# Graph attention sums: the value rows of all four heads are weighed by one VectorE operation, and ScalarE keeps only the exponentials

## The reference, cut to what matters

```python
m = jax.ops.segment_max(score, col_idx, num_segments=n)
ex = jnp.exp(score - m[col_idx])
denom = jax.ops.segment_sum(ex, col_idx, num_segments=n)
alpha = ex / denom[col_idx]
agg = jax.ops.segment_sum(alpha[..., None] * msg_edge, col_idx, num_segments=n)
```

## Time and profile before

| | us |
|---|---|
| median of 3 runs | 4174.1 (4173.09 to 4183.92) |
| the profiled execution's own time | 4177.06 |
| its span, first to last instruction | 4175.2 |
| PE busy | 3149.1 (75%) |
| DVE busy | 2234.4 (54%) |
| ACT busy | 894.9 (21%) |
| POOL busy | 2743.4 (66%) |

### The profile page before, as it was taken

How to read it: one execution, slowest core, us unless ns; L and a number is a source line. 1 busy time by engine, 2 the same in 40 slices (tenths; PEclk the granted TensorE clock), 3 DMA queues, 4 the chain that set the end, 5 groups by cost and what they waited for, 6 DMA issues and landing times. The chain is left out here.

```text
span 4175.2 us, 64203 instructions
## 1 busy us (share of the span) xinstructions
PE 3149.1 (75%) x11666; PEld 2153.8 (52%) x11666; DVE 2234.4 (54%) x7572; ACT 894.9 (21%) x2584; POOL 2743.4 (66%) x2879
## 2 busy tenths in 40 slices
PE   5999938777788873786788878888786776767763
PEld 2444426556566652333667767777544444444442
DVE  8200037666666646333788868776654433444435
ACT  1333300000200000342344456555320000100000
POOL 3777767777677775234777767777217777477774
PEclk9999959999999986998887769877888877788876
DMA  4333323333333334566555546555213333333332
GB/s 142 142 145 151 142 73 105 106 105 105 95 105 106 106 107 131 217 257 233 165 165 165 164 129 176 163 162 162 66 50 106 105 105 106 99 106 105 105 106 90
DMA packets 226896, 540.00 MB, mean 129 GB/s; under 512 B 73482, under 2 KB 107948, under 8 KB 212876
## 3 DMA queue, kind: packets, MB, share of 16 engines
q0 software_dynamic: 136528, 374.97, 30.1%
q1 hardware_dynamic: 57880, 103.46, 6.8%
q10 hardware_dynamic: 32164, 57.91, 4.7%
HBM read 390.04 MB, written 146.09 MB: 128 GB/s over the span
## 5 line engine op out<-in xcount | busy, mean ns | idle before, releaser
L604 POOL DMA_INDIRECT gcn_edges_g<-table,rows_i x782 | 740.3, 947 | 434.3 <-ACTq L875 196.7
L923 PE MATMUL ps<-gcn_edges_g,gcn_edges_onehot 128*128 x1760 | 627.8, 497 | 309.1 <-SPq L620 271.4
L969 DVE TENSOR_TENSOR acc<-acc,ps 128x256 f32 (+1 forms) x880 | 370.0, 420 | 750.6 <-PE ps L923 740.3
L923 PEld LDWEIGHTS ps<-gcn_edges_g,gcn_edges_onehot 128*128 128x128 f32 x1760 | 392.2, 242 | 537.3 <-issue 484.5
L307 POOL DMA_INDIRECT records<-rec,slots x391 | 375.9, 961 | 184.1 <-issue 124.2
L604 POOL DMA_INDIRECT score_g<-table8v,rows_i x391 | 380.2, 972 | 131.0 <-issue 110.6
L604 POOL DMA_INDIRECT rel_g<-table,rows_i x391 | 371.8, 951 | 134.7 <-issue 96.9
L604 POOL DMA_INDIRECT score_g<-table8k,rows_i x391 | 371.4, 950 | 135.0 <-issue 109.4
L604 POOL DMA_INDIRECT conv_edges_g<-table,rows_i x391 | 371.7, 951 | 127.3 <-issue 93.8
L359 PE MATMUL ps<-w,xt 128*128 128x512 f32 x1000 | 435.8, 595 | 18.3 <-ACT xt L329 18.3
L1047 PE MATMUL ps<-q,onehot_t 128*128 x880 | 322.8, 503 | 109.6 <-DVE onehot_t L1146 108.3
(11 more groups left out here) (319 smaller groups left out, 4768.6 us busy)
## 6 DMA issues: line engine op xcount, KB each, us to landing
table<-tb SPq DMA_DIRECT2D x50, 1280.0 KB, 4.5
score_dst_bc<-dst_rows ACTq DMA_DIRECT2D x110, 256.0 KB, 3.5
sum_dst_bc<-dst_rows ACTq DMA_DIRECT2D x110, 256.0 KB, 3.4
gcn_edges_g<-table,rows_i POOLq DMA_INDIRECT x782, 2.8
table<-gcn_tb SPq DMA_DIRECT2D x50, 128.0 KB, 1.7
records<-rec,slots POOLq DMA_INDIRECT x391
rel_g<-table,rows_i POOLq DMA_INDIRECT x391, 2.8
conv_edges_g<-table,rows_i POOLq DMA_INDIRECT x391, 2.8
```

Of the source, the lines that this page charges most:

```text
L604: pool.indirect_dma_start(out=m.g[:, 2 * slot_of(p) + j, 0:D], out_offset=None, in_=table, in_offset=bass.IndirectOffsetOnAxis(ap=m.rows_i ...
L923: mm = pe.matmul(bank(m, i % BANKS, 0, width), m.onehot[:, 2 * k + j, :], window(m.g, slot + j, 0, width), start=(j == 0), stop=(j == 1))
L969: nc.vector.tensor_tensor(acc, acc, bank(m, i % BANKS, 0, width), ALU.add).then_inc(added, 1)
```

## The change

DVE's `weigh` now takes the whole 256 columns of each row, with all four weights, in one operation. ACT's four multiplications for each item, its wait for the arrival of the rows, its registers that held the slot in the ring, and the semaphore `by_act` with PE's wait on it are gone. Nothing else is changed.

```diff
@@ tensor
                 pe.wait_ge(onehot_ready, i - 1)
                 pe.wait_ge(by_dve, i - 1)
-                pe.wait_ge(by_act, i - 1)
                 pe.wait_ge(added, i - 1)
@@ scalar
         act.wait_ge(added, 1)
-        regs = ItemRegisters(act, m, "sum")
         for i in range(SPREADS - 2):
...
             kk = i % UNROLL
-            slot = regs.slot(i)
             act.wait_ge(multiplied, i + 1)
             act.wait_ge(diff_ready, i + 3)
             nc.scalar.activation(vx[:, kk, :, D:ACCW], diff[:, i % 2, :].rearrange("p (j h) -> p j h", j=2),
                                  ACT.Exp).then_inc(exp_ready, 1)
-            act.wait_ge(exp_ready, i + 1)
-            act.wait_ge(m.arrived, regs.need(i))
-            for j in (0, 1):
-                for h in ACT_HEADS:
-                    ins = nc.scalar.activation(vx[:, kk, j, h * DK:(h + 1) * DK],
-                                               window(m.g, slot + j, h * DK, (h + 1) * DK), ACT.Copy,
-                                               scale=vx[:, kk, j, D + h:D + h + 1])
-            ins.then_inc(by_act, 1)
-            regs.load(i + 1)
-        regs.free()
@@ vector
         def weigh(i):
             kk = i % UNROLL
-            rows = m.g[:, bass.ds(regs.slot(i), 2), 0:2 * DK]
+            rows = m.g[:, bass.ds(regs.slot(i), 2), 0:D]
             dve.wait_ge(exp_ready, i + 1)
             dve.wait_ge(m.arrived, regs.need(i))
             heads = lambda v: v.rearrange("p j (h d) -> p j h d", d=DK)
-            nc.vector.tensor_tensor(heads(vx[:, kk, :, 0:2 * DK]), heads(rows),
-                                    vx[:, kk, :, D:D + 2].rearrange("p j (h o) -> p j h o", o=1).to_broadcast([P, 2, 2, DK]),
+            nc.vector.tensor_tensor(heads(vx[:, kk, :, 0:D]), heads(rows),
+                                    vx[:, kk, :, D:ACCW].rearrange("p j (h o) -> p j h o", o=1).to_broadcast([P, 2, HEADS, DK]),
                                     ALU.mult).then_inc(by_dve, 1)
```

More of the change, by code:

```diff
@@ L1244, in attention_sum @@
     gather = next_gather(ctx, nc, m, "sum")
-    (spread_ready, onehot_ready, max_spread, diff_ready, exp_ready, by_act, by_dve, multiplied, added) = sems(
+    (spread_ready, onehot_ready, max_spread, diff_ready, exp_ready, by_dve, multiplied, added) = sems(
         ctx, nc, "sum", "spread_ready", "onehot_ready", "max_spread", "diff_ready", "exp_ready",
-        "by_act", "by_dve", "multiplied", "added")
+        "by_dve", "multiplied", "added")
     loaded = sems(ctx, nc, "sum", *(f"loaded{k}" for k in range(SPREADS // 2)))
-    m.spent += [spread_ready, onehot_ready, max_spread, diff_ready, exp_ready, by_act, by_dve, multiplied, added, *loaded]
-    ACT_HEADS = (2, 3)
+    m.spent += [spread_ready, onehot_ready, max_spread, diff_ready, exp_ready, by_dve, multiplied, added, *loaded]
     def sync(sp):
```

## The result

| | before | changed |
|---|---|---|
| median of 6 runs each, us | 4174.65 (4168.78 to 4183.92) | 4199.56 (4195.51 to 4202.6) |
| span of the profiled execution, us | 4175.2 | 4198.5 |

The ratio is 1.0059 with a 95% interval of 1.0049 to 1.007: the kernel became 24.9 us slower, where 18.4 were foretold.

What follows compares the result with a forecast made beforehand. POOL's issuing in the sums was taken as the bound; start -0.3, longer issues +18.4 and tail +0.3 gave +18.4 us, 4195.5 on the profiled execution's 4177.06, 4192 against the runs, range 4178 to 4206.

Steps and rivals of the forecast that it cites:

- POOL's issuing is the bound; ACT's relief is worth nothing.: Stretch of the sums: POOL's issues pace it, 1.28 us for each of 359 tiles; removing PE's 37.8 us of waits gains 0.
- The weighing costs 689 ns and DVE's turn has room.: DVE in the sums: weighing grows by 262 to 689 ns, covered because DVE's turn stays under POOL's 2.27 us; cost 0.
- Each issue is held until the operands have been streamed, 0.552 us with 512 columns.: POOL's issues in the sums: held until 0.29 us after a weighing's start with 256 columns, 0.552 us with 512.
- The Trainium skill's inference: POOL's issues beside DVE's weighing: by it they would stay at 975 ns and the sum be 0 instead of +18.4.
- that page's lock for the whole instruction: DVE's weighing against POOL: blocked time would be 427 and 689 ns, giving +24.4 us.
- +18.4 us by hits at random.: POOL's issues in the sums: average delay grows from 19.6 to 70.9 ns, 51.3 ns more for each of 359 issues.
- a turn becomes 1.89: DVE's turn with nothing idle in the sums: from 1.63 to 1.89 us, still under POOL's 2.27, margin 0.38 us.
- upper bound without a lock: POOL's issues in the sums: the whole 25 ns grow with the square of the operation's length, +23.5 us.
- Start -0.3 and tail +0.3.: Ends of the sums: POOL's first release 0.3 us earlier, DVE's last weighing delaying the end by 0.3 us.
- Rival A: POOL's issues in the sums aren't slowed and nothing changes: 4174 to 4186 us (0 to 12 us); chance 0.26.
- Rival B: Sums held by ACT, PE's largest releaser with 37.8 us, so the change is faster: 4149 us; chance 0.06.
- Rival C: DVE or the ring becomes the bound in the sums: at most 58 us, 4232; chance 0.05.

Runs made afterwards that it cites:

- experiment 1: Changed kernel with DVE's weighing cut back to heads 0 and 1 (128x256), heads 2 and 3 left out as zeros: 4171.94 us beside 4174.85, ratio 0.9993.
- experiment 2: Changed kernel with the weights for the 512-column weighing in PSUM, ACT writing the exponentials twice: 4165.85 us beside 4174.85, ratio 0.9976.
- 12: Changed kernel with the weighing as two operations of 256 columns instead of one of 512: 4184.32 us beside 4176.59, ratio 1.002.
- Experiments 4 and 11: Changed kernel with an unused subtraction added to each DVE turn: 128 columns (4) 4175.19 us, 32 columns (11) 4205.0 us.
- runs 5 to 10: Changed kernel with fillers or halved weighing, and kernel before with three heads on DVE, where POOL's issuing isn't the bound: ratios 0.9928 to 0.9992.

## Why the prediction was right

*POOL's issuing is the bound; ACT's relief is worth nothing.* Right. The stretch from release to last issue carries the whole difference, and without the longer operation the time is that of before (experiment 1).

*The weighing costs 689 ns and DVE's turn has room.* Right: 692, and no wait for the ring appears. But the turn at full ring came out at 1.70 us where 1.89 was said. The step to 1.89 added the whole growth to a turn in which DVE had a gap that the longer weighing takes up. Experiment 1, without ACT's multiplications and with the short weighing, has the same turn of 1.63 as the earlier trace rows, so the gap is not ACT's pace:

```profile
2514.61 0.16 DVE L1322 TENSOR_TENSOR diff<-scores,ps 128x8 f32<-128x8 f32 x1
2514.91 0.42 DVE L1331 TENSOR_TENSOR vx<-score_g,vx 128x256 f32<-128x256 f32 x1
```

and the changed kernel:

```profile
2508.41 0.15 DVE L1322 TENSOR_TENSOR diff<-scores,ps 128x8 f32<-128x8 f32 x1
2508.54 0.69 DVE L1331 TENSOR_TENSOR vx<-score_g,vx 128x512 f32<-128x512 f32 x1
```

From the start of the difference to that of the weighing it is 0.30 us there and 0.13 here, or 0.07 in the turns beside. With 0.27 more for the weighing and some 0.2 less for the gap, 1.63 becomes 1.70. What fills the gap with the short weighing stays open.

*Each issue is held until the operands have been streamed, 0.552 us with 512 columns.* Right in form and nearly in size: 0.57 in the timeline. The second SBUF operand is shown as the cause by experiment 2, and the growth with the length of one operation by 12. The Trainium skill's inference ("SBUF — State Buffer", section "Who interferes with whom") that `tensor_tensor` doesn't stall a DMA issued from GpSimd doesn't hold for the indirect issues of this kernel (1051 ns with two SBUF operands, 959 with one), as the prediction said; another kind of issue was not run. As for that page's lock for the whole instruction, POOL is held for 0.57 us of the 692 ns recorded. But the records of DVE overlap: the add begins 0.61 us behind the weighing (2505.14 and 2505.75 above), so the held time isn't far from the time in which the weighing has DVE to itself.

*+18.4 us by hits at random.* The term that was mis-sized: it measured 27.7. With an empty ring the formula holds, 58 ns for 51. With a full ring DVE's turn of 1.70 us lay between POOL's 1.25 and 1.25 + 0.57, and the two locked one to one for five to seven issues at a time; these 80 us gave 10.1 us where the formula gives 55 x 51 ns = 2.8. Hits at random at a turn of 1.70 instead of 2.15 us would explain an estimated 1 us of that. The turn of 1.89 that the prediction reckoned with would not have locked, so its step "a turn becomes 1.89" is what hid this. Experiments 4 and 11 show the lock by moving the turn to either side of 1.82: 4175 and 4205 us. The prediction named a lock only as a reason for "more", without a size. Its upper bound without a lock, +23.5 us on 4174.1, is 4197.6 and lies under the 4199.56 measured; the range holds the result by what it allowed for locking on top.

*Start -0.3 and tail +0.3.* POOL's run began 3.6 us earlier and the tail was 1.4 us shorter; the first is mostly the scatter of the stages before, by the 3.1 us at the first weighing, the second wasn't followed up. Both are small beside the rest.

*Rival A* (no growth, within 0.3%) fell with 1051 ns. *Rival B* (ACT was the bound) is refuted by experiment 1 where POOL's issuing is the bound. Whether it holds in part in the world of runs 5 to 10 was not shown. *Rival C* (DVE or the ring as the bound) fell: DVE was idle for 62 us waiting for rows.

The best version is neither of the two kernels: with one operand of the weighing in PSUM the kernel takes 4166 to 4167 us, 8 to 9 us less than before, with four heads on DVE or with two.

## What to carry to other kernels

Where GpSimd's DMA issuing paces a stage, look at every VectorE operation beside it that reads two SBUF tensors: on this kernel it held an indirect issue that came behind it, for 0.29 us with 256 columns and 0.57 us with 512. By the estimate for hits at random, which gave 51 ns where 58 were measured, the loss grows with the square of the length of one operation. Put one operand into PSUM, or cut the operation into pieces. And compare the two periods: if VectorE's turn lies between GpSimd's free period and that period plus the held time, issue after issue can run into the next operation, and a little more or a little less work on VectorE moves the time either way.

## What had not been expected

Adding an unused 128-column operation to each turn of a DVE that was already busy for 58.2 of 60 us (2500 to 2560) took 24 us off the changed kernel, since a turn of 1.875 us falls in step with three issues of 1.25 us to two turns. An issue that comes 0.02 us ahead of a two-operand operation or 0.60 us behind its start takes 0.94 or 0.95 us, as if alone.
